# Router tasks four to a slot and expert scatters two to a step in an attention and expert kernel

## The reference

```python
x = x + _L0_xattn_ref(ctx_768, _layernorm(x), mask, ...)       # 4 heads of 64, RMS norm on q and k
x = x + _L0_ffn_ref(_layernorm(x), gate_w, gate_bias, w_gate, w_up, w_down)

# _L0_ffn_ref, E, K, G, TG, CAP = 64, 8, 8, 4, 256
scores = sigmoid(x @ gate_w.T)
sfc = scores + gate_bias                  # best 4 of 8 groups, then the best 8 of 64 experts
topk_idx = top_k(where(smask, sfc, -inf), K)[1]
topk_w = scores at topk_idx, divided by their sum, times 2.5
pos = rank of the row among those of its expert, in the order of the rows
buf = zeros((E, CAP + 1, h)).at[e, where(pos < CAP, pos, CAP)].set(x[token])[:, :CAP]
y = silu(buf @ w_gate) * (buf @ w_up) @ w_down
out = zeros((n, h)).at[token].add(y[e, pos] * topk_w * (pos < CAP))
```

## Time and profile before

| what | value |
|---|---|
| time, median of 3 runs | 1085.38 us (1082.44 to 1087.95) |
| the profiled execution, first to last instruction | 1168.4 us |
| its difference to the median | 83.0 us longer |
| attention, from the first step to the last | 84 to 817 us |
| last router tasks and scatters | 817 to 877 us |
| experts and the joining of the planes | 877 to 1168 us |
| PE, DVE, ACT, POOL busy | 906.8, 655.7, 463.0, 581.3 us |

### The profile page before, as it was taken

One profiled execution on the slowest core, in us unless ns is written; L12 is line 12 of the kernel. 1 busy time (PEld: TensorE's weight loads), 2 busy tenths in 40 slices (PEclk: granted clock), 3 DMA queues, 4 the chain that ended last, 5 costly groups with the idle time before them and its releaser, 6 DMA issues.

```text
span 1168.4 us, 13234 instructions
## 1 busy us (share of the span) xinstructions
PE 906.8 (78%) x3848; PEld 626.7 (54%) x3848; DVE 655.7 (56%) x1956; ACT 463.0 (40%) x930; POOL 581.3 (50%) x522
## 2 busy tenths in 40 slices
PE   3869999999999999999964973957308999889300
PEld 2545666556656656656532542846207888777200
DVE  4475647875789775888652743743533443333206
ACT  3734675545755646664430521333103333222000
POOL 3530231204755635655665073155554888888850
PEclk9879999999999999999986995968658999999755
DMA  7739602012221422101261102000428999999689
GB/s 249 267 111 386 218 3 72 20 31 90 77 78 58 132 84 87 55 23 67 78 239 54 37 29 87 24 24 9 171 88 244 308 312 188 158 159 152 70 231 392
DMA packets 85335, 150.77 MB, mean 129 GB/s; under 512 B 14090, under 2 KB 53050, under 8 KB 83216
## 3 DMA queue, kind: packets, MB, share of 16 engines
q1 hardware_dynamic: 54543, 112.32, 27.8%
q0 software_dynamic: 30720, 37.61, 16.3%
HBM read 69.19 MB, written 97.45 MB: 143 GB/s over the span
## 4 chain that ended last, share of the span: by engine, by line
PE 48%; DVE 13%; issue 11%; POOL 8%; another core or an unknown queue 7%; DMA 7%; ACT 4%; POOLq 0%; SPq 0%; ACTq 0%; DVEq 0%
PE ps_o L1257 15%; PE ps_u L1154 6%; POOL sum L1111 4%; PE ps_s L1233 4%; PE ps_s L1235 4%; PE ps_u L1177 4%; DMA out_rows<-again,row_ids 3%; PE ps_u L1269 2%; PE ps_o L1252 2%; POOL out_rows L1111 2%; PE ps_u L1321 2%; DVE mp L1580 2%; PE ps_u L1165 2%; DMA sum<-again,row_ids 2%
## 5 line engine op out<-in xcount | busy, mean ns | idle before, releaser
L1044 POOL DMA_INDIRECT slot_rows<-rows,slot_idx x256 | 251.2, 981 | 312.0 <-issue 137.5
L1580 DVE TENSOR_REDUCE mp<-ps_u 128x1 f32<-128x512 f32 x256 | 165.1, 686 | 103.2 <-remote 49.6
L1450 ACT ACTIVATE probs<-ps_s 128x512 f32<-128x512 f32 x256 | 139.9, 596 | 176.6 <-PE ps_s L1235 105.4
L1111 POOL DMA_INDIRECT sum<-again,row_ids x84 | 130.0, 1548 | 26.5 <-issue 22.6
L1257 PE MATMUL ps_o<-probs,pool 128*128 128x512 f32 (+1 forms) x288 | 138.0, 602 | 2.5 <-ACT den L1471 2.5
L1321 PE MATMUL ps_u<-again 128*128 128x256 f32 x512 | 123.9, 386 | 0.0
L1257 PE MATMUL ps_o<-probs,V 128*128 128x512 f32 (+1 forms) x216 | 106.4, 615 | 10.4 <-ACT probs L1453 5.9
L1235 PE MATMUL ps_s<-qbT,Kb 65*128 65x512 f32 (+1 forms) x252 | 102.4, 406 | 0.0
L1752 DVE TENSOR_SCALAR again<-ps_o,again 128x256 f32<-128x256 f32 x128 | 56.1, 480 | 82.3 <-DMA sum<-again,row_ids 54.7
L1154 PE MATMUL ps_u<-wqkv_s,lnT 128*128 128x512 f32 (+1 forms) x256 | 97.4, 515 | 4.1 <-ACT lnT L1373 3.2
L1321 PEld LDWEIGHTS ps_u<-again 128*128 128x128 f32 x512 | 94.2, 194 | 11.0 <-issue 0.3
(11 more groups left out here) (190 smaller groups left out, 1610.8 us busy)
## 6 DMA issues: line engine op xcount, KB each, us to landing
again<-in_wexp SPq DMA_DIRECT2D x64, 384.0 KB, 5.3
slot_rows<-rows SPq DMA_DIRECT2D x2, 10272.0 KB, 35.0
again<-slot_rows SPq DMA_DIRECT2D x64, 321.0 KB
sum<-rows SPq DMA_DIRECT2D x2, 4352.0 KB, 27.6
again<-sum SPq DMA_DIRECT2D x8, 1024.0 KB, 11.3
Kb<-K SPq DMA_DIRECT2D x16, 275.5 KB
pool<-in_x SPq DMA_DIRECT2D x4, 1024.0 KB, 5.5
xres<-in_x SPq DMA_DIRECT2D x8, 512.0 KB
```

The lines of the kernel that those rows point to most:

```text
L1044: pool.indirect_dma_start(out=slot_rows, out_offset=bass.IndirectOffsetOnAxis(ap=slot_idx[x][:, q, k:k + 1], axis=0), in_=rows[x][:, q, :] ...
L1111: pool.indirect_dma_start(out=(out, *sums)[e % PLANES], out_offset=bass.IndirectOffsetOnAxis(ap=row_ids[:, e % RING, t:t + 1], axis=0), in ...
L1450: act.activation(probs[:, n % NPR, hh, :], ps_s[:, u % NSC, :], ACT.Exp).then_inc(s["probs_made"], 1)
L1580: v.tensor_reduce(mp[:, i, tile, half:half + 1], bank((*t, i))[:, :], AX.X, ALU.max).then_inc(s["emptied_vec"], 1)
```

## The change

The change has two parts, both in the plan; no instruction is added or taken away, save the waits of the scatters that are paced.

First, `route`. Before, the routers of halves (0, 0) to (2, 0) were chained through `put`, mostly one task to a slot and later where an engine was full; only that of (2, 1) was put four tasks to a slot. Now all six are put four tasks to a slot, from the fifth slot of the next half on, and their cost is booked in `self.load`. The scatters stand one to a slot behind them.

Second, `paced`. Before, the scatters of halves (0, 0) to (1, 1), number n = 0 to 3, waited for step 18 (n + 2) and then went two to a step; those of (2, 0) and (2, 1) waited for no step. Now the first six halves, n = 0 to 5, wait from step 18 (n + 1) + 9 on, two to a step: half a half earlier than before for the first four, and paced for the next two. Those of the last batch stay unpaced.

```diff
@@ -102,6 +102,8 @@
+SCATTER_LAG = 9
@@ -272,17 +274,12 @@
     def route(self, half, first):
         b, x = half
         tasks = self.route_tasks(b, x)
-        if half < (B - 2, 1):
-            self.chain(tasks, first, [(("scale", b, x, PR - 1, 1), 1)])
-            first = self.at[tasks[-1]] + 1
-        else:
-
-            for n, t in enumerate(tasks):
-                self.slots.setdefault(first + n // 4, []).append(t)
-            first += len(tasks) // 4
-
-        first = max(first, self.last_scatter)
-        pace = 1.0 if half < (B - 2, 1) and x else 0.5
+        for n, t in enumerate(tasks):
+            self.slots.setdefault(first + n // 4, []).append(t)
+            for e, c in COST[t[0]].items():
+                self.load[(e, first + n // 4)] = self.load.get((e, first + n // 4), 0.0) + c
+        first = max(first + len(tasks) // 4, self.last_scatter)
+        pace = 1.0
         for n in range(QT * TOPK):
             self.last_scatter = first + int(pace * n)
@@ -528,8 +525,8 @@
     def paced(self, b, x, q, k):
 
-        if (b, x) < (B - 2, 0):
-            return NKT * PR * (2 * b + x + 2) + (TOPK * q + k) // 2
+        if (b, x) < (B - 1, 0):
+            return NKT * PR * (2 * b + x + 1) + SCATTER_LAG + (TOPK * q + k) // 2
```

## The result

| | before | changed |
|---|---|---|
| time, median | 1085.29 us (1082.44 to 1087.95, 4 runs) | 1100.07 us (1099.41 to 1101.65, 4 runs) |
| ratio, with its 95% interval | 1 | 1.0138 (1.0117 to 1.0159) |
| span of the profiled execution | 1168.4 us | 1099.9 us |

The changed kernel is slower by 14.8 us, 1.1 us beyond the upper end of my range. The forecast itself, 1089 us, was 11 us too low. The profiled execution went the other way: 68.5 us shorter. Its own time is 1101.65 us, and the span of 1099.9 us fits that: the changed kernel's profile holds no lost time that its timed runs lack.

A forecast was written before the change was run, and what follows sets the result against it. PE was taken to bound the first six halves, POOL with little or no slack the end in timed runs. 1085.4 + 0 + 0 + 0 + 4 = 1089 us; range 1074 to 1099, likeliest case 1086 to 1094.

The forecast's parts named there:

- term 1: Routers of the first six halves four to a slot: 0 us, bounds -5 and +15.
- The rival of the packed router: Choice tasks on DVE delay the reductions PE needs to free `ps_u`: slower, 1099 us (1098 to 1104), chance 0.18.
- Term 4: Three scatters of (2, 1) between those of (3, 0) delay POOL's bias add and later scatters: +4 us, up to +7.
- Term 2: Scatters of the first four halves nine steps earlier: 0 us, bounds -2 and +4.
- Term 3: Scatters of (2, 0) and (2, 1) paced: 35 to 55 us off the profile's span, timed runs 0, bound -13.
- most of it is lost only while the profiler records: Some 90 us lost in 597 to 817 us, close to the 83.0 us between profile and median, mostly absent from timed runs.
- about 18 us by the lower clock: Cost of PE's lower clock in the bursts of (2, 0) and (2, 1), beside 22.4 + 20.9 us idle.
- the lost time is partly real: Rival: timed runs lose time in scatter bursts too and pacing returns it: faster, 1077 us (1070 to 1083), chance 0.24.
- The rule of the Trainium skill: DVE and GpSimd share ports, so routers moved off other scatters would gain; within -4 and +2 per half, sum unmoved.
- the two slow instructions of the earlier trace: Two DVE choice instructions, read as beside scatters: 2034 and 2608 ns, against 225 and 178 ns in the comparison rows.
- the 4.2 us: DVE time in one router that the prediction said goes to POOL's work: some 4.2 us.

The follow-up runs named there:

- e1: Routers of the first six halves four to a slot, scatters and paces as in the kernel before: 1176.9 us, against 1171.5 for the kernel before on its chip.
- e9: The router-only kernel (first six halves four to a slot, scatters as before) on another chip: 1168.4 us, against 1161.9 for the kernel before there.
- e13: The router-only kernel (first six halves four to a slot, scatters as before) on another chip: 1174.3 us, against 1170.9 for the kernel before there.
- e17: The router-only kernel (first six halves four to a slot, scatters as before) on another chip: 1167.2 us, against 1161.7 for the kernel before there.
- e8: Changed kernel with all scatters of (2, 1) ahead of those of (3, 0), still paced: 1096.7 us, against 1086.0 for the kernel before on its chip.
- e5: The changed kernel unaltered, run again on chip 14: 1102.1 us, against 1086.0 for the kernel before there, ratio 1.0136.
- e6: Kernel before, with rows that found no place written to spare rows instead of dropped, chip 14: 1089.9 us, against 1086.0 for the kernel before.
- e12: The changed kernel unaltered, on a chip where the kernel before takes 1161.9 us: 1134.2 us, ratio 0.9752.
- e11: Kernel before, with unplaced rows written to spare rows, on a chip where the kernel before takes 1161.9 us: 1162.4 us, ratio 0.9987.
- e14: Router-only kernel with the first five routers two tasks to a slot instead of four: 1168.7 us, against 1170.9 for the kernel before on its chip.

## Why the prediction was wrong

**The step that failed is term 1**, "the router four to a slot", which I took at 0. The first six halves take 10.5 us more (513.1 and 523.6), and e1, e9, e13 and e17 show that the router alone makes about 9 us of it (500.9 and 509.8 to 510.5 us up to the last steps of the sixth half). The bound I gave, +15, held; the value did not. I had chosen it by the nearest row, the router of (2, 1), with PE busy for 96% around it, and had written down the reason against it myself: that half has no keys beside it. The row was near in density and far in what shares DVE.

The rival of the packed router (0.18, 1099 us) was the one that came true: slower, PE busy for 501.7 of 523.4 us between 84 and 607.4, half starts that drift, if only from the fourth half on (345.8, 434.1, 522.2 and 607.4 us against 345.4, 427.1, 518.4 and 597.1). Its place was half right. I had expected PE to wait for banks of `ps_u` behind line 1580, and put the sign of it at 10 us more of such waits. It waits for row maxima instead, 7.1 us at line 1201 (4.7 for those of middle blocks, 2.4 for those of the next half), and only 1.8 us more in all: four fifths of the changed kernel's loss are not waiting at all but the clock at its lower level for 3.4 to 6.8 us behind such waits. By idle time alone I would have found a sixth of it. I had used the clock for the disturbed stretches and not for term 1. That its 1099 us came within 1.1 us of the result is partly luck, as its 9 to 15 us were priced for another wait.

**Term 4**, three scatters late at the end, +4: the size was right. e8 takes them away and gains 5.4 us; the bias add is 4.1 us later with them. The reason was right in half: POOL does have slack behind the bias add, 8.6 us of waits, but the router of (3, 1) is put off with it. I had taken +0 for a router that bounds the end, and it bounds it here at +4.

**Term 2**, the first four halves' scatters nine steps earlier, 0: not separated from the rest, but the router-only runs leave at most 1 us for it: up to the last steps of the sixth half they take 509.8 to 510.5 us, the changed kernel 509.2 to 510.7. (The overlap is seven steps and nine, not six and nine.)

**Term 3**, the paces of (2, 0) and (2, 1): my reading that "most of it is lost only while the profiler records" was wrong. A loss of about this size is in every timed run on four of the five chips, and in none on the fifth nor in the measurement of the change; the profile of before came from an execution with them and the median from runs without. For the runs that were timed the term was small, as I had said: on kind A the last two halves take 141.5 us in e5 and 145.8 in e6 (before, but for the spare rows), 4.3 us less, within my bound of -13. Of the "about 18 us by the lower clock", the rows of the two bursts give 10.6 (17.6 us at 0.71 and 22.1 at 0.75). The profiled span was to fall to 1110 to 1140 us; it fell to 1099.9 because the other kind of chip was read. On kind B, in e12, it is 1128.2, and there the change wins 27.7 us. The rival "the lost time is partly real" was thus right for the chips of kind B and wrong for those on which the change was measured.

The sum, on chip 14, from the first step to the last scatter: e5 takes 721.9 us and e6 711.8. Of the 10.1 us, the first six halves make 10.3 (523.4 and 513.1), the last two -4.3 and the scatters behind them 4.1 (57.0 and 52.9). e6 is 3.9 us slower than the kernel before, which gives 14.0, against 16.1 measured on this chip and 14.8 in the first measurement. It does not close better than that, for one profile is one execution. That the first six halves of e6 take as long as those of before is chance: its fourth half has some 3.5 us more, by the spare rows, and its second 3.2 us less (92.1 us; 95.3 before and in e11, which is the same kernel as e6), as the lower-clock stretches that before and e11 have near 228 and 248.5 us are missing in e6. And e6 reaches its first step 3.3 us earlier than e5, where executions of the changed kernel alone differ by as much (80.3 us in e12, 84.0 in e5).

The rule of the Trainium skill that I weighed did not move the sum, but I had read my rows wrongly: the two slow instructions of the earlier trace rows did not stand beside scatters alone. The first of them (line 1660, at 486.4 us) and the second (line 1727, at 514.1) run while POOL does sums and products of its own (line 1077 and others). The same DVE instruction twice in the changed kernel, with what POOL did:

```profile
286.07 2.56 DVE L1655 TENSOR_TENSOR rep<-sfc 128x128 f32<-128x128 f32 x1
286.59 1.90 POOL L1056 TENSOR_TENSOR pool<-pool,rs_y 128x1024 f32<-128x1024 f32 x1
...
388.43 1.12 POOL L1041 DMA_INDIRECT slot_rows<-rows,slot_idx  x1 [0.30 <-issue]
388.74 0.29 DVE L1655 TENSOR_TENSOR rep<-sfc 128x128 f32<-128x128 f32 x1
```

Beside a scatter it takes 0.29 us, as beside an idle POOL (202.9 us); beside POOL's TENSOR_TENSOR it takes 2.56, and 0.70 us twice (466.4 and 560.8). By the Trainium skill (SBUF — State Buffer, section Who interferes with whom) a DVE instruction with two inputs in SBUF contends with a GpSimd instruction that reads SBUF. The trace agrees for POOL's TENSOR_TENSOR, and shows no such price for a scatter alone: in the profiles of before, the change, e5, e12 and e17, none of 1141 such DVE instructions beside a scatter alone took over 0.25 us more than its shortest case, while 186 of 275 beside a TENSOR_TENSOR of POOL did. Where POOL's sum follows right behind a scatter, DVE can be stopped already during the scatter (at 486.4 us, 0.6 us ahead of POOL's product). So most of the 4.2 us go to POOL's sums and products for the keys. They reach PE, too: behind the 2.56 us stands the reduction at 291.3 for whose bank PE waited 2.0 us, ahead of the lower clock from 293.2 on. How much of the 9 us comes this way was not measured.

## What to carry to other kernels

A packed run of small instructions on one engine is dangerous by what stands behind it, not by its sum: look for the last instruction of each chain that another engine waits for (here the maximum over the parts, 0.35 us of work), and try to keep it ahead of the run (no run here did). Price a new wait of TensorE with the clock that it can lose afterwards: here 16.8 us more at the lower clock cost 8.4 us where idle time grew by 1.8. When a disturbed stretch hides a comparison, look for the last step ahead of it that both kernels share: read up to there, e14 and the runs of the router alone said what their times could not. And where the span of a profile and the timed runs differ by 7%, ask first whether they come from the same chip and time, and put both cases to the forecast.

## What the runs showed of the hardware

The same program had two times on different chips of this type, each used at one time: 1085 to 1086 us and 1162 to 1171 us for the kernel before. The difference shows in stretches in which a dozen or more indirect scatters of POOL follow one another 1.28 us apart: waits of DVE and ACT that no instruction of the core ends then last up to 25 us (e17 has 50.2 us of such waits at one line of DVE), while the scatters start as far apart as on the other chips. Two scatters to a step of the attention did not show it. Whether the rows are dropped or stored makes no difference (e11). The cause was not found.

A DVE instruction with two inputs took 0.29 us beside an indirect scatter of POOL and beside an idle POOL, and 0.70 to 2.56 us beside a TENSOR_TENSOR of POOL.

Lower-clock stretches of 3.4 us come and go between executions of one kernel: e11 has those near 228 and 248.5 us and e6 doesn't, and the half around them takes 95.3 and 92.1 us.
